# The node pass of a four-layer graph network written anew: centred weights, bias added by POOL, three PSUM banks a product, squares on ScalarE

## The reference, cut to what matters

```python
e = silu(edge_in @ eW1 + eb1)
e = silu(e @ eW2 + eb2)                       # 128 features an edge
agg = segment_sum(e, row, num_segments=n)     # "sums2" in the kernel
node_in = concatenate([h, agg], axis=1)
out = silu(node_in @ nW1 + nb1) @ nW2 + nb2   # the node pass
x = layernorm(x + out)                        # the node pass too
```

## Time and profile before

| | |
|---|---|
| median of 3 runs | 4799.02 us (4790.83 to 4802.06) |
| the profiled execution: its own time | 4836.87 us |
| its span, first to last instruction | 4835.2 us |
| mean granted TensorE clock in it | 0.703 of full speed |
| busy: PE, PEld, DVE, ACT, POOL | 3475.6, 2837.2, 2155.2, 1390.9, 2850.0 us |
| node pass, first load issued to first DMA of the next pass | 3235.5 to 3609.9 us |

### The profile page before, as it was taken

One profiled execution on the slowest core, in us unless ns is written; L12 is line 12 of the kernel. 1 busy time (PEld: TensorE's weight loads), 2 busy tenths in 40 slices (PEclk: granted clock), 3 DMA queues, 4 the chain that ended last, 5 costly groups with the idle time before them and its releaser, 6 DMA issues. The chain is left out here.

```text
span 4835.2 us, 72365 instructions
## 1 busy us (share of the span) xinstructions
PE 3475.6 (72%) x19803; PEld 2837.2 (59%) x19803; DVE 2155.2 (45%) x5433; ACT 1390.9 (29%) x3272; POOL 2850.0 (59%) x2834
## 2 busy tenths in 40 slices
PE   4665537766777537776677998779977777777778
PEld 3342127766333236675577667767746677766778
DVE  8999923342899412223322223424542222622225
ACT  1110002222455401112222564434432222222235
POOL 1778867775677767775577660001127776277753
PEclk9776755555799855555688999989985555755559
DMA  4002312112688731112665785545652111311115
GB/s 132 3 3 80 125 32 55 53 48 76 225 330 329 265 128 27 27 27 98 227 178 153 250 255 174 184 167 203 233 193 86 27 27 25 125 27 27 27 39 185
DMA packets 311487, 589.50 MB, mean 122 GB/s; under 512 B 178785, under 2 KB 180702, under 8 KB 292960
## 3 DMA queue, kind: packets, MB, share of 16 engines
q1 hardware_dynamic: 146819, 465.93, 27.1%
q0 software_dynamic: 87808, 66.01, 6.6%
q10 hardware_dynamic: 76506, 53.12, 3.4%
HBM read 286.68 MB, written 310.95 MB: 124 GB/s over the span
## 5 line engine op out<-in xcount | busy, mean ns | idle before, releaser
L1286 PE MATMUL e_ring<-e_msgs,e_hot 128*128 x6272 | 1387.7, 422 | 574.7 <-DVEq L1158 574.7
L1286 PEld LDWEIGHTS e_ring<-e_msgs,e_hot 128*128 128x128 f32 x6272 | 1352.1, 332 | 611.9 <-issue 611.9
L1035 POOL DMA_INDIRECT e_msgs<-y,index_D x784 | 740.0, 944 | 341.1 <-issue 220.9
L1150 DVE TENSOR_TENSOR e_hot<-e_nodes,keys_D 128x2048 f32<-128x2048 f32 x147 | 336.8, 2291 | 1107.3 <-SPq L1074 1087.0
L611 POOL DMA_INDIRECT list_S<-s_place,s_target x392 | 439.8, 1122 | 216.2 <-issue 119.2
L611 POOL DMA_INDIRECT list_D<-d_place,d_target x392 | 385.5, 983 | 161.5 <-issue 119.0
L1593 POOL DMA_INDIRECT m_far<-x,index_S x392 | 382.5, 976 | 154.1 <-issue 114.3
L1035 POOL DMA_INDIRECT e_msgs<-y,index_S x392 | 386.8, 987 | 135.3 <-issue 117.4
L1035 POOL DMA_INDIRECT e_msgs<-x_by_relation,index_D x392 | 373.0, 951 | 134.7 <-issue 109.1
L2441 POOL TENSOR_TENSOR n_sq<-n_cent 128x1792 f32<-128x1792 f32 x14 | 44.4, 3173 | 671.9 <-DVE n_cent L2336 671.9
L1384 ACT ACTIVATE rows_late<-e_ring,dinv 128x64 f32<-128x64 f32 x784 | 171.5, 330 | 757.0 <-PE e_ring L1286 757.0
(11 more groups left out here) (395 smaller groups left out, 5453.9 us busy)
## 6 DMA issues: line engine op xcount, KB each, us to landing
x_by_relation<-d_stage SPq DMA_DIRECT2D x98, 1024.0 KB, 5.3
m_keyrow<-keys_by_step SPq DMA_DIRECT2D x49, 512.0 KB, 4.6
rows<-pairs_by_edge SPq DMA_DIRECT2D x49, 512.0 KB, 4.7
messages<-rows SPq DMA_DIRECT2D x98, 256.0 KB
rows<-messages SPq DMA_DIRECT2D x49, 512.0 KB, 4.2
sums<-m_stage ACTq DMA_DIRECT2D x98, 256.0 KB, 3.6
n_in<-sums SPq DMA_DIRECT2D x14, 1792.0 KB, 8.2
s_xc<-x_padded SPq DMA_DIRECT2D x28, 448.0 KB, 3.7
```

The source lines that it names most:

```text
L1035: pool.indirect_dma_start(out=msgs[:, (i % HELD) * D:(i % HELD + 1) * D], out_offset=None, in_=source, in_offset=bass.IndirectOffsetOnAxis ...
L1150: nc.vector.tensor_tensor(hot[g % 2][:, :, :], bc(nodes[:, 0:P].unsqueeze(1), [P, GS, P]), bc(order["keys"][:, g * GS:(g + 1) * GS].unsque ...
L1286: mm = nc.tensor.matmul(ring[:, bass.ds(bucket, D)], hot[g % 2][:, k, :], msgs[:, bass.ds(tile, D)], start=False, stop=False, skip_group_c ...
```

## The change

`node_pass` does one thing now (the other kinds weren't used). In words:

- nW2 (`wn2`) and nb2, the latter now broadcast to 128 partitions (`spread["n2"]`), are centred along the output features in `order_sources`, as further entries of `K["centred"]`. The sum x2 + out then has mean zero, so the pass takes no mean and subtracts none. The split of the bias in three is gone, and so is the bias matmul.
- POOL adds the bias to the loaded x2 rows in place (`biased`), a chunk ahead, and multiplies by dinv for y3 (`scaled`), which DVE did. ACT squares (`square`, after quad 2's SiLU), which POOL did.
- p_1, p_o, u and flat_a have three buffers (NB; u had two, flat_a seven), p_a two.
- SP waits for each of the three loads by itself, sums first, and issues them behind the stores of the chunk before last but one; x3 is stored as soon as it is ready, y3 after it.
- All 98 quads are written out.

```diff
@@ order_sources
-            nc.vector.memset(K["ones3"][:, :], 1.0)
-            for parts, to in biases:
...
-                rest = parts[0]
-                for r in range(3):
-                    step(nc.vector.tensor_copy(part16[:, :], rest[:, :]))
...
-                step(nc.vector.tensor_copy(to[:, :, :], bc(kept[:, :].unsqueeze(1), [3, QUAD, D])))
@@ gnn
-        K["centred"] = ((0, P, by_row(wall[:, :]), REL), (0, P, by_row(spread["2"][:, :]), 1),
+        K["centred"] = ((0, P, by_row(wn2[:, :]), 1), (0, P, by_row(spread["n2"][:, :]), 1),
+                        (0, P, by_row(wall[:, :]), REL), (0, P, by_row(spread["2"][:, :]), 1),
...
-                 (bias["n2"][:, :], nb2.partition_broadcast(3)), (spread["1"][:, :], b1.partition_broadcast(P)),
+                 (spread["n2"][:, :], nb2.partition_broadcast(P)), (spread["1"][:, :], b1.partition_broadcast(P)),
@@ node_pass, sync
+            def load(c):
+                h = c % 2
+                if c >= 2:
+                    sp.wait_ge(s_turn, NQ * (c - 1))
+                sp.dma_start(summed[h][:, :, :].rearrange("p t f -> p (t f)"), of_chunk(sums, c, HID)
+                             ).then_inc(s_summed[h], 16)
+                if c >= 2:
+                    sp.wait_ge(s_first, NQ * (c - 1))
+                sp.dma_start(turned[h][:, :], of_chunk(x2t, c, D)).then_inc(s_turned[h], 16)
+                if c >= 2:
+                    sp.wait_ge(s_value, NQ * (c - 1))
+                sp.dma_start(rows[h][:, :, :].rearrange("p t f -> p (t f)"), of_chunk(x2, c, D)).then_inc(s_rows[h], 16)
+            def store(c):
+                h = c % 2
+                sp.wait_ge(s_x3, c + 1)
+                sp.dma_start(of_chunk(x3, c, D), result[h][:, :, :].rearrange("p t f -> p (t f)")).then_inc(s_out[h], 16)
+                sp.wait_ge(s_y3, c + 1)
+                sp.dma_start(of_chunk(y3, c, D), scaled[h][:, :, :].rearrange("p t f -> p (t f)")).then_inc(s_out[h], 16)
+            load(0)
+            load(1)
+            for c in range(CHUNKS):
+                if c >= 1:
+                    store(c - 1)
+                if c + 2 < CHUNKS:
+                    load(c + 2)
@@ node_pass, tensor: turn and first_product as flip and first_product before, b = k % 2 and k % NB
+                if n == 0:
+                    pe.wait_ge(s_summed[c % 2], 16 * (c // 2 + 1))
...
+                if n == 0:
+                    pe.wait_ge(s_turned[h], 16 * (c // 2 + 1))
...
             def second_product(k):
-                nc.tensor.matmul(p_o[b][:, 0:QUAD, :], K["ones3"][:, :], weights["b"][:, :, :],
-                                 start=True, stop=False)
+                b = k % NB
+                pe.wait_ge(s_u, k + 1)
+                if k >= NB:
+                    pe.wait_ge(s_value, k - NB + 1)
+                for j in range(QUAD):
+                    mm = nc.tensor.matmul(p_o[b][:, j, :], u[b][:, slot(j)], weights["W"][:, :], start=True, stop=True)
@@ node_pass, scalar
+            for k in range(QUADS):
+                b = k % NB
+                if k + 1 < QUADS:
+                    flat_out(k + 1)
+                act.wait_ge(s_first, k + 1)
+                if k >= NB:
+                    act.wait_ge(s_second, k - NB + 1)
+                nc.scalar.activation(u[b][:, :], p_1[b][:, :], ACT.Silu, bias=weights["b1"][:, 0:1]).then_inc(s_u, 1)
+                if k >= NQ and k % NQ == 2:
+                    square(k // NQ - 1)
+                if k >= NQ and k % NQ == 4:
+                    root(k // NQ - 1)
@@ node_pass, gpsimd
+            biased(0)
+            for c in range(CHUNKS):
+                h = c % 2
+                if c + 1 < CHUNKS:
+                    biased(c + 1)
+                pool.wait_ge(s_x3, c + 1)
+                if c >= 2:
+                    pool.wait_ge(s_out[h], 32 * (c // 2))
+                nc.gpsimd.tensor_tensor(scaled[h][:, :, :], result[h][:, :, :],
+                                        bc(K["dinv"][:, c * CH:(c + 1) * CH].unsqueeze(2), [P, CH, D]), ALU.mult
+                                        ).then_inc(s_y3, 1)
@@ node_pass, vector: add(k) as out_of before, but it waits at n == 0 for s_biased, s_x3 and s_sq
+            for k in range(QUADS):
+                add(k)
+                if k >= NQ and k % NQ == 3:
+                    variance(k // NQ - 1)
+                if k >= NQ and k % NQ == 5:
+                    norm(k // NQ - 1)
```

More of the change, by code:

```diff
@@ L2184, in sem @@
             return sems[-1]
[L2186 to L2193, removed]
+        rows = [sb(f"rows{h}", [P, CH, D]) for h in range(2)]
+        turned = [sb(f"turned{h}", [P, CW]) for h in range(2)]
+        summed = [sb(f"summed{h}", [P, CH, HID]) for h in range(2)]
+        flat_a = [sb(f"flat_a{b}", [HID, QE]) for b in range(NB)]
+        value = [sb(f"value{h}", [P, CH, D]) for h in range(2)]
+        result = [sb(f"result{h}", [P, CH, D]) for h in range(2)]
+        scaled = [sb(f"scaled{h}", [P, CH, D]) for h in range(2)]
+        sq = sb("sq", [P, CH, D])
+        var = sb("var", [P, CH])
+        std = sb("std", [P, CH])
+        rstd = sb("rstd", [P, CH])
+        u = [sb(f"u{b}", [HID, QE]) for b in range(NB)]
+        p_a = [ps(f"p_a{b}", [HID, QE]) for b in range(2)]
+        p_1 = [ps(f"p_1{b}", [HID, QE]) for b in range(NB)]
+        p_o = [ps(f"p_o{b}", [P, 2 * QUAD, D]) for b in range(NB)]
+        s_rows = [sem(f"rows{h}") for h in range(2)]
+        s_turned = [sem(f"turned{h}") for h in range(2)]
+        s_summed = [sem(f"summed{h}") for h in range(2)]
         s_out = [sem(f"out{h}") for h in range(2)]
+        s_biased = sem("biased")
         s_turn = sem("turn")
[L2196 to L2201, removed]
+        s_flat = sem("flat")
+        s_first = sem("first")
+        s_u = sem("u")
+        s_second = sem("second")
+        s_value = sem("value")
         s_sq = sem("sq")
@@ L2204, in node_pass @@
         s_std = sem("std")
+        s_rstd = sem("rstd")
         s_x3 = sem("x3")
[L2206 to L2234, removed]
+        s_y3 = sem("y3")
@@ L2235, in node_pass, with of_chunk @@
         inner = ctx.enter_context(ExitStack())
         block = inner.enter_context(nc.Block())
-        stores = 3 if kind == "conv2" else len(outs) + (copy is not None)
-        def place(i, k):
-            return i * NS + k, i * 2 + k // NQ, (k // NQ) % 2, k % 2, k % NQ
-        def slot(j):
-            return slice((j % 2 * 2 + j // 2) * P, (j % 2 * 2 + j // 2 + 1) * P)
+        def of_chunk(table, c, width):
+            return table.rearrange("(p t) f -> p (t f)", p=P)[:, c * CH * width:(c + 1) * CH * width]
@@ L2634, in node_pass @@
+            variance(CHUNKS - 1)
+            norm(CHUNKS - 1)
         inner.close()
```

447 lines of the change are left out of this document (90 added, 357 removed).

## The result

After the change the median is 4752.42 us (4 runs, 4750.0 to 4755.61), beside 4800.54 us (4 runs, 4790.83 to 4805.57) for the kernel before on the same chip. The ratio of the comparison is 0.9879, with a 95% interval of 0.983 to 0.9928: faster. By the medians it is 48.1 us, where 43.2 were forecast (4756 for 4752.4).

The account below looks back on a forecast made before the run. PE's sequence of 98 quads at one pitch was taken to bound the node pass. Terms -33.3 + 3.0 - 4.1 - 8.8 = -43.2 us took the median from 4799.0 to 4756 us, range 4742 to 4780.

Parts of the forecast that it names:

- Part 1: Second product in the node pass: without the bias matmul the pitch falls from 3.41 to 3.06 us, -33.3 us.
- The rival of 0.21 a quad: Second product: removing the bias matmul saves only 0.21 us, the weight load stays exposed; 4769 us, chance 0.09.
- Part 2: Root on ACT: PE stalls 0.25 us at quad 5 in 12 chunks, +3.0 us; third banks worth nothing.
- The rule of the double cost of a table switch: ACT's root: by the Trainium skill a switch costs about 2.66 us, not 1.31; stall 1.6 us, 16 us less gain.
- Part 3: Square on ACT, scaling and biasing on POOL: costs nothing; first add of a chunk 3.2 us late, 4.9 left.
- that rival: Square on ACT needs its own table, two loads of 1.28 us more a chunk; 4761 us, chance 0.10.
- Part 4: Loads and stores: sums have 11.6 us to land, hidden; sums first at the start saves 4.1 us.
- The rival named the right limit: Loads landing beyond 11.6 us cost half a us each a chunk; 4773 us, chance 0.08; nothing left, 0.04.
- Part 5: Behind the last matmul: shorter chain of add, square, scaling and y store, -8.8 us (bounds -6 and -10).
- the slower rival: PE's clock falls through the short new stalls; 4825 us at 20% of the pass at low level, chance 0.05.
- Part 6: Set-up: nine small DVE steps go and six come, covered by POOL's scatter; nothing, without cover under 1 us gain.
- The 4793.7 for a profiled execution: Whole kernel: forecast time of a profiled execution, the sum of -43.2 us taken off the 4836.9 us before.

Follow-up runs that it names:

- e2: Kernel after the change, plus one bf16 matmul of three rows and 64 columns a quad, written to unused columns: 4777.14 us, pitch 3.333 us.
- e3: Kernel after the change, plus one bf16 matmul of 128 rows and 256 columns a quad, written to unused columns: 4759.94 us, pitch 3.117 us.
- e4: Kernel after the change, plus one fp32 matmul of 128 rows and 64 columns a quad, written to unused columns: 4772.58 us, pitch 3.229 us.
- e5: Kernel after the change, with two buffers instead of three of p_1, p_o, u and flat_a: 4745.12 us, pass 327.30 us.
- e1: Kernel after the change, with the three-row bias matmul put back before each second product, its moving operand zero: median 4788.07 us, ratio 0.9977 to the kernel before.
- e7: Kernel after the change, with the x2 rows loaded ahead of sums and turned rows in every chunk: 4805.87 us, pass 331.09 us.

## Why the prediction was right, point by point

**What bounds the pass** held. PE stayed the bound, at granted clock 1.00 from the second quad on, and each kernel's pass is its pitch times 98, its stalls, a start and a tail.

**Part 1, the bias matmul** was right in its mechanism, and the gain was forecast some 14% too small: 95 x 0.408 = 38.8 us for 33.3. The step that was mis-sized is the pitch without it, forecast at 3.06 and measured at 3.005. Of the forecast 0.35 a quad, 0.30 is the time from L2592's last start to L2614's first less 0.216, and that came as it was forecast (0.10 + 0.20). The other 0.05 is the weight load exposed behind the bias, which was read from durations (0.32 us for the first L2614, 0.28 for the rest), whose ends are modelled. By the starts it is 0.10: the second L2614 is 0.16 behind the first with the bias matmul and 0.06 without, and from the second product's start to the next turn it is 0.95 and 0.84. 95 times the missing 0.055 are 5.2 of the 5.5 us. What exposes the two loads the prediction left open; e2 and e3 name the three rows. The rival of 0.21 a quad fell.

**Part 2, the root's stall** came in the quad forecast and for the reason given, 12 x 0.36 = +4.3 us for +3.0. Counted from the start of its iteration (3243.48), the SiLU of quad 5 ends at 5.38, as in before (5.37), and the second product starts at 5.43. It was due at 3.005 + 2.17 = 5.17; that is 0.26, and the exposed load is 0.10 here too: 0.36. The forecast had 5.23 and 0.05, so both its misses are those of Part 1 again. The same sum gives 5.43 + 0.10 - 5.40 = 0.13 for e4 (pitch 3.229), whose stall is 0.137. The copy of quad 6 ends at 3.38, in time for L2247's start at its usual 0.44 (3246.93) but too late to load its weights ahead, so that L2247 takes 1.11 instead of 1.02; this 0.09 lies within the wait for SiLU and adds nothing. The rule of the double cost of a table switch is not borne out: the copy ends at 3246.86, the load starts at 3246.87 for 1.28 and SiLU at 3248.17, so a switch cost 1.31 again. That the third bank can't help was right (e5).

**Part 3** cost nothing, as forecast. Square took 1688 ns in the median on ACT and no table of its own: that rival fell. All fourteen, by their group:

```profile
L2277 ACT ACTIVATE n_sq<-n_value x14: 1687/1688/1697, 3237.4 to 3510.0; 128x1792 f32<-128x1792 f32 x14
```

One size was off. POOL's two operations a chunk, by their groups (ns shortest, median, longest; first and last start; then the waits of others for the first):

```profile
L2313 POOL TENSOR_TENSOR n_rows<-n_rows,spread_n x14: 3976/3987/3996, 3209.0 to 3491.4; 128x1792 f32<-128x1792 f32 x14
...
  DVE n_value L2340: 78.5, 12
```

```profile
L2324 POOL TENSOR_TENSOR n_scaled<-n_result,dinv x14: 3189/3191/3195, 3252.8 to 3516.6; 128x1792 f32<-128x1792 f32 x14
```

The scaling is 3.19 us as taken from the earlier trace rows, the bias 3.99 instead of the same 3.19. The first add of a chunk is therefore some 4.0 us late instead of 3.2 (x3 at 3.0, scaling 3.2 and bias 4.0 into the boundary iteration), and DVE waits 78.5 us in 12 such adds; PE waits for none of them, as 4.9 us were free.

**Part 4, the loads.** For chunk 2 the boundary iteration begins at 3249.85, and SP's queue shows:

```profile
3256.07 0.32 SPq L2211 DMA_DIRECT2D y<-n_scaled  x1
3256.44 0.43 SPq L2197 DMA_DIRECT2D n_summed<-sums  x1
```

The sums are issued 6.6 us into it (forecast 6.8), and the sixth turn behind it starts at 3267.87, so they had 11.4 us (forecast 11.6) and PE never waited for them. When they land, the trace of after doesn't tell; in e1, whose loads stand in the same order, the sums issued behind stores land 8.5 us behind their issue in four of the five cases that its trace has, 9.3 in the fifth. So some 3 us were to spare, as forecast (an estimate from e1's 8.5 and the 11.4). How near that is to the limit e7 shows, where eight of eleven are late with 896 KB more ahead. The rival named the right limit, and the loads kept short of it; its price of half a us for each us beyond wasn't measured by itself. The start gave 13.20 - 8.82 = 4.4 us for the 4.1; but 0.8 of it goes again, for the quad that used to run while the clock was already up now runs below it (L2249's four take 1.91 in after at a granted clock of 0.50, L2592's took 1.18). Net 3.6. The prediction had no term for that. The second line of the table above adds up with it: 38.8 - 4.3 - 0.8 = 33.7, and 327.14 - 293.44 = 33.70.

**Part 5, the tail**: 34.10 - 25.64 = 8.5 us for 8.8, and term by term: last add -0.1 for -0.2, from it to the square -6.3 for -6.2, Square -1.5 for -1.5, scaling +1.2 for +1.3, issue of the y store -0.4 for -0.4, from there to the next pass 6.0 instead of 7.5, -1.5 for -1.8. The last chunk of after, all engines:

```profile
3500.23 0.61 PE L82 MATMUL n_p_a<-ident,n_summed 128*128 128x128 f32 x4
...
3509.57 0.42 DVE L2340 TENSOR_TENSOR n_value<-n_p_o,n_rows 128x256 f32<-128x256 f32 x1
3510.02 1.70 ACT L2277 ACTIVATE n_sq<-n_value 128x1792 f32<-128x1792 f32 x1 [3.51 <-DVE n_value L2340]
...
3516.62 3.19 POOL L2324 TENSOR_TENSOR n_scaled<-n_result,dinv 128x1792 f32<-128x1792 f32 x1 [3.70 <-DVE n_result L2354]
3519.84 0.32 SPq L2211 DMA_DIRECT2D y<-n_scaled  x1
...
3525.87 3.42 SPq L1042 DMA_DIRECT2D rows_late<-y  x7
```

The last add ends at 9.8 behind the start of iteration 96, the square begins 0.03 behind it, and the chain add, Square, variance, root, reciprocal, norm, scaling, store follows without a gap of another chunk's work.

**The clock** stayed at 1.00 in the windows; the slower rival fell. The stalls of 0.36 us didn't lower it.

**Part 6** can't be told by itself, and no run isolates it. In the twelve traces without a long scatter the pass begins at 3193.8 to 3200.1 us in three kernels made from before, and at 3189.7 to 3199.1 in nine made from after, so it isn't more than a few us either way.

Terms against measured, in us: -33.3 / -38.8; +3.0 / +4.3; -4.1 / -3.6; -8.8 / -8.5; sum -43.2 / -46.6, and the pass by its ends -46.5. The errors in size, 5.5 one way and 1.3 + 0.5 + 0.3 the other, have opposite signs, so that the sum comes nearer to the pass than its largest term does; that is luck. So is the 4756 beside 4752.4, as far as it is nearer than the scatter of the runs. The 4793.7 for a profiled execution (4755.6) rested on one of before with a long scatter and says nothing.

## What to carry to other kernels

On a bound PE, look at what a small matmul does to its neighbours' starts, not at its own duration: one with three rows cost 0.41 us a quad here, and padding it to 128 rows took nearly three quarters of that away (26 of the 46 us of the pass). Read what a load costs from the distance of two starts; read from durations it came out at half here, and that put two terms wrong. A stall of an engine that feeds PE is a question of due times; it moves with the pitch, so that each gain on PE has to be followed by a new reckoning of who is just in time (the root one quad later gave 5 us). Read the length of the pass from the trace when other stages scatter by more than the change is worth.

## What the runs showed of the hardware that wasn't expected

- Weights of three rows between weights of 128 put loads in the open on both sides: the pitch rose by 0.33 us with 64 columns and 0.41 with 256, beside 0.11 for 128 rows of bf16 and 256 columns. Why few rows do this no trace says, nor whether fp32 does it too.
- POOL's elementwise square of 128x1792 took 4.76 instead of 3.17 us where a DVE operation on two operands in SBUF overlapped it for 1.74 us; DVE lost nothing.
- POOL's operation on 128x1792 took 3.17 us with the same tile twice, 3.19 with dinv repeated along the innermost axis and 3.99 with a row of 64 repeated along the tiles, the last with DVE standing still (it waited for it). The first two multiply and the last adds, so whether the pattern or the operation makes the difference is open.
- Behind 28 turns that took 6.15 us the following ones ran at the upper level from their first (eight in 1.09 us instead of 1.97).
